# Forward transforms of two spectral layers: column units placed between the next group's row units

## The reference, cut to what matters

```python
x_ft = jnp.fft.rfft2(gn(x))          # layer 0: 16 of the 33 half-spectrum columns and 28 rows are used
mix(x_ft[:, :, :K2, :MODES_T], w[0]) # ... and three more blocks of 6 to 8 rows
...
x_f = jnp.fft.rfft2(gn(x))           # layer 3: the whole half spectrum
out_f = jnp.einsum('bchw,ochw->bohw', x_f, k_f)
```

## Time and profile before

| what | us |
| --- | --- |
| median of three runs | 924.1 (920.47 to 928.2) |
| span of the profiled execution | 904.1 |
| median less the span | 20.0 |
| layer 0's transform: first product's result read, to the next stage's first product | 153.89 to 218.05 |
| layer 3's transform: first product, to the end of its last copy | 616.79 to 710.18 |

### The profile page before, as it was taken

One profiled execution on the slowest core, in us unless ns is written; L12 is line 12 of the kernel. 1 busy time (PEld: TensorE's weight loads), 2 busy tenths in 40 slices (PEclk: granted clock), 3 DMA queues, 4 the chain that ended last, 5 costly groups with the idle time before them and its releaser, 6 DMA issues. The chain is left out here.

```text
span 904.1 us, 27651 instructions
## 1 busy us (share of the span) xinstructions
PE 755.6 (84%) x11429; PEld 633.2 (70%) x11429; DVE 586.3 (65%) x1097; ACT 456.1 (50%) x768; POOL 86.2 (10%) x80
## 2 busy tenths in 40 slices
PE   7999997785599667876799999958888498988996
PEld 7999996674588546665344444428777388888996
DVE  3554464777847745887786777776666676765445
ACT  0133336775343305652699995007887556775200
POOL 0000000010010002644022313000000100000000
PEclk9999998998899987997999999988999898999998
DMA  8599878862110000000000000004000447860036
GB/s 309 205 344 350 317 217 253 186 137 43 27 31 0 0 2 1 0 0 1 1 1 2 1 1 1 1 1 95 0 0 0 93 95 162 175 128 1 1 142 236
DMA packets 48668, 80.52 MB, mean 89 GB/s; under 512 B 20034, under 2 KB 38472, under 8 KB 43736
## 3 DMA queue, kind: packets, MB, share of 16 engines
q1 hardware_dynamic: 31960, 62.75, 25.0%
q10 hardware_dynamic: 16640, 16.78, 5.4%
HBM read 51.01 MB, written 27.92 MB: 87 GB/s over the span
## 5 line engine op out<-in xcount | busy, mean ns | idle before, releaser
L1588 DVE SCALAR_TENSOR_TENSOR X<-bank,c_power,X 32x512 f32 x128 | 96.8, 756 | 36.5 <-PE bank L1538 32.8
L1731 PE MATMUL bank<-m_xp,m_kf 128*32 128x64 f32 x2048 | 82.7, 248 | 22.2 <-DVE m_xp L1666 11.1
L1731 PEld LDWEIGHTS bank<-m_xp,m_kf 128*32 128x32 f32 x2048 | 81.4, 171 | 23.5 <-issue 23.5
L220 DVE BATCH_NORM_STATS2 bn<-X 128x6 f32 x128 | 83.1, 683 | 2.9 <-POOL X L1328 1.6
L420 DVE COPY ks_rows<-bank 128x512 f32<-128x512 f32 x64 | 41.2, 687 | 66.6 <-PE bank L350 66.6
L438 ACT COPY ks_spec<-bank 128x512 f32<-128x512 f32 x64 | 34.4, 589 | 97.4 <-PE bank L365 97.4
L1494 ACT ACTIVATE c_r<-X,c_nrm 32x1024 f32 (+1 forms) x56 | 74.9, 1337 | 2.4 <-DVE c_nrm L1562 1.1
L350 PE MATMUL bank<-ks_fw,ks_src 64*128 64x64 f32 x1024 | 68.7, 298 | 6.3 <-DMA ks_src<-in_L_conv_weights 6.3
L350 PEld LDWEIGHTS bank<-ks_fw,ks_src 64*128 64x128 f32 x1024 | 68.1, 215 | 6.2 <-issue 6.2
L365 PE MATMUL bank<-ks_fh,ks_rows 64*128 64x128 f32 (+1 forms) x1152 | 71.5, 279 | 0.0
L365 PEld LDWEIGHTS bank<-ks_fh,ks_rows 64*128 64x128 f32 (+1 forms) x1152 | 67.0, 183 | 2.6 <-issue 1.8
(11 more groups left out here) (183 smaller groups left out, 1683.5 us busy)
## 6 DMA issues: line engine op xcount, KB each, us to landing
ks_src<-in_L_conv_weights SPq DMA_DIRECT2D x16, 1024.0 KB, 7.0
kf<-ks_spec ACTq DMA_DIRECT2D x16, 1024.0 KB, 9.2
m_kf<-kf SPq DMA_DIRECT2D x32, 512.0 KB, 8.5
X<-in_x SPq DMA_DIRECT2D x4, 2048.0 KB, 12.6
out_y<-X SPq DMA_DIRECT2D x32, 256.0 KB, 2.6
xf<-l_y SPq DMA_DIRECT2D x24, 112.0 KB, 2.1
l_wb<-in_L_conv_weights_r SPq DMA_DIRECT2D x4, 512.0 KB, 11.5
l_wb<-in_L_conv_weights_i SPq DMA_DIRECT2D x4, 512.0 KB, 13.4
```

Of the source, the lines that this page charges most:

```text
L220: dve.bn_stats(self.bn[:, c, :], self.X[:, q, c * CH:(c + 1) * CH]).then_inc(step, 1)
L1588: dve.scalar_tensor_tensor(x, of.rearrange("p (y x) -> p y x", x=HN), filt.power[at, 2:3], x, ALU.mult, ALU.add).then_inc(added, 1)
L1731: last = pe.matmul(ps[4 * half + m // 8][at:at + C, m % 8 * N:(m % 8 + 1) * N], kf[p][:, j, :, H * half + m], xp[half][:, j, m].rearrange( ...
```

## The change

A group's column units no longer follow its row units at once. All units of the four groups are put in one list, in which column unit `s` of a group follows the next group's row units by two places. In layer 3 the list begins with eleven row units, goes on with one column and one row in turn, and ends with ten column units (the last two of group 2 and all of group 3). In layer 0 it is eleven row units, then one column unit for every two row units, and five column units at the end (the last of group 2 and the four of group 3).

`f_rows` is there twice. `f_src`, `f_th` and `f_tl` are rings of four units, and `f_ch`, `f_cl` are gone: column units use the same rings. Each engine goes through the list; on ACT and DVE the copy out of the bank of unit n - 4 stands ahead of unit n. Everything is written out without loops.

The normalisation of a chunk goes to POOL, apart from the first group's first three chunks (DVE, DVE, ACT) and, in layer 0, chunk 2 (DVE) and chunk 6 (ACT) of the other groups. Row copies go to ACT for units 1 and 5 in layer 0, 3 and 7 in layer 3, and otherwise to DVE. In layer 3 ACT's copy into `xm` writes four neighbouring elements at a time, where it wrote single ones 32 elements apart.

```diff
-    def __init__(self, pr, ctx, name, mats, slot_at, rows_by_act, norm_by_act, norm_by_dve):
+    AHEAD = 3
+    RING = 4
+    def __init__(self, pr, ctx, name, mats, slot_at, rows_by_act, normal_by):
+        per = NCH // self.S
+        place = {(0, q, j): 2 * (NCH * q + j) for q in range(Q) for j in range(NCH)}
+        place |= {(1, q, s): 2 * (NCH * q + NCH + per * s + 2) + 1 for q in range(Q) for s in range(self.S)}
+        self.units = sorted(place, key=place.get)
...
+        self.src = pr.sb(ctx, f"{name}_src", [P, self.RING, CH])
+        self.th, self.tl = (pr.sb(ctx, f"{name}_{n}", [P, self.RING, CH], F16) for n in ("th", "tl"))
+        self.rows = [pr.sb(ctx, f"{name}_rows{p}", [P, N, 2, 4 * self.S]) for p in range(2)]
...
+    def wait_source_free(self, eng, q, j):
+        m = NCH * q + j - self.RING
+        if m >= 0:
+            eng.wait_ge(self.turned, self.at[0, m // NCH, m % NCH] + 1)
...
+        def multiply(n):
+            kind, q, i = self.units[n]
+            pe.wait_ge(self.turned_read, n + 1)
+            if n >= 4:
+                self.wait_evicted(pe, n - 4)
...
+        turned = 0
+        for n in range(len(self.units)):
+            while turned < min(n + self.AHEAD + 1, len(self.units)) and self.rows_before(turned) <= n:
+                turn(turned)
+                turned += 1
+            multiply(n)
...
+    def normalise(self, eng, e, q, j):
+        pr = self.pr
+        if q >= Q or self.normal_by(q, j) != e:
+            return
+        self.wait_source_free(eng, q, j)
+        to, of = self.src[:, (NCH * q + j) % self.RING], pr.X[:, q, j * CH:(j + 1) * CH]
+        scale, shift = pr.rstd[:, q:q + 1], pr.shift[:, q:q + 1]
+        if e == "act":
+            m = eng.activation(to, of, ACT.Identity, scale=scale, bias=shift)
         else:
+            m = eng.tensor_scalar(to, of, scale, shift, ALU.mult, ALU.add)
+        m.then_inc(self.ready[e], 1)
...
+        for n, (kind, q, i) in enumerate(units):
+            for m in range(evicted, max(evicted, self.rows_before(n), n - self.AHEAD)):
+                evict(m)
+            evicted = max(evicted, self.rows_before(n), n - self.AHEAD)
+            act.wait_ge(self.turned, n + 1)
+            if n >= self.RING:
+                act.wait_ge(self.made, n - self.RING + 1)
...
-                for q in range(Q):
-                    for s in range(S):
-                        pool.wait_ge(fwd.kept, START + S * q + s + 1)
-                        pool.tensor_tensor(xm[q % 2][:, 1, s, :, 0, :],
+                for j in range(fwd.RING):
+                    fwd.normalise(pool, "pool", 0, j)
+                for kind, q, i in fwd.units:
+                    if kind == 0:
+                        fwd.normalise(pool, "pool", *divmod(NCH * q + i + fwd.RING, NCH))
+                    else:
+                        pool.wait_ge(fwd.kept, S * q + i + 1)
+                        pool.tensor_tensor(xm[q % 2][:, 1, i, :, 0, :],
...
-                fwd.high_parts(act, lambda q, s: act.copy(
-                    xm[:, s, :, :, bass.ds(IB * q, IB)].rearrange("p k r b -> p b r k"),
-                    pr.psum[4 + s % 4][:].rearrange("p (b r k) -> p b r k", b=IB, r=2)))
+                fwd.high_parts(act, lambda q, s, bank: act.copy(
+                    xm[:, s, :, :, IB * q:IB * q + IB], bank[:].rearrange("p (b r k) -> p k r b", b=IB, r=2)))
```

More of the change, by code:

```diff
@@ L476, in __init__ @@
[L476 to L484, removed]
+        self.ready = {e: pr.sem(f"{name}_ready_{e}") for e in ("act", "dve", "pool")}
+        self.rows_read = {e: pr.sem(f"{name}_rows_read_{e}") for e in ("act", "dve")}
@@ L495, in product @@
             return pe.matmul(to, l, m[:, 0], start=False, stop=True)
-        pe.sem_inc(self.turned, START)
-        self.pr.keep_warm(pe, 7)
[L499 to L536, removed]
-            for s in range(S):
[L538 to L602, removed]
-        else:
-            for q in range(Q - 1):
-                group(q, True)
-        group(Q - 1, False)
@@ new lines, in multiply @@
+        def multiply(n):
+            kind, q, i = self.units[n]
+            pe.wait_ge(self.turned_read, n + 1)
+            if n >= 4:
+                self.wait_evicted(pe, n - 4)
+            bank, th, tl = ps[4 + n % 4], self.th[:, n % self.RING], self.tl[:, n % self.RING]
+            for k in range(4):
+                at = slice(k * P, (k + 1) * P)
+                w = width if kind else self.RW
+                m = product(bank[:, k * w:(k + 1) * w], th[:, at], tl[:, at], self.fh if kind else self.fw)
+            if kind and i == 0 and self.fh0 is not None:
+                for b in range(IB):
+                    at = slice(b * P, b * P + C)
+                    m = product(bank[0:C, b * width:(b + 1) * width], th[:, at], tl[:, at], self.fh0)
+            m.then_inc(self.made, 1)
@@ new lines, in high_parts, with evict @@
+    def high_parts(self, act, keep):
+        ps, units = self.pr.psum, self.units
+        def evict(n):
+            kind, q, i = units[n]
+            self.copy_rows(act, "act", act.copy, n)
+            if kind:
+                act.wait_ge(self.made, n + 1)
+                keep(q, i, ps[4 + n % 4]).then_inc(self.kept, 1)
+        for j in range(NCH):
+            if j < self.RING:
+                self.normalise(act, "act", 0, j)
+        evicted = 0
+        for n, (kind, q, i) in enumerate(units):
[3 more added lines that the diff above has]
+            act.wait_ge(self.turned, n + 1)
+            if n >= self.RING:
+                act.wait_ge(self.made, n - self.RING + 1)
+            if kind == 0:
+                act.copy(self.th[:, n % self.RING], ps[n % 4][:]).then_inc(self.high, 1)
+                self.normalise(act, "act", *divmod(NCH * q + i + self.RING, NCH))
+            else:
+                act.copy(self.th[:, n % self.RING].rearrange("p (b s c) -> p s b c", b=IB, s=4),
+                         ps[n % 4][:].rearrange("p (s b c) -> p s b c", s=4, b=IB)).then_inc(self.high, 1)
+        for n in range(evicted, len(units)):
+            evict(n)
@@ L711, in _, with keep @@
             def _(act):
-                def keep(q, s):
+                def keep(q, s, bank):
                     if s == 0 and q >= 2:
```

126 lines of the change are left out of this document (79 added, 47 removed).

## The result

The changed kernel takes **896.0 us** (median of 4, 883.61 to 899.71) against 925.27 for the kernel before on the same chip: ratio 0.961, 95% interval 0.953 to 0.969. Faster, and by more than I forecast: 29 us by the medians where the sum had 23, and 36 by the ratio, which leaves out the longer of a kernel's executions. The steps that led to the forecast were off by more, in both directions.

A forecast was written before the change was run, and what follows sets the result against it. No engine is full; time is lost at seams between phases and in phases another engine paces. Span 904.1 less 12.1 (layer 3) and 10.9 (layer 0) is 881.1, plus 20.0 around it 901.1 us; range 893 to 915.

The forecast's parts named there:

- The 20.0 that lie around it: Whole execution: 20.0 us lie around the span, added to the forecast span of 881.1.
- A gain of 12.1 us: Layer 3's forward transforms: 93.4 us before, 81.3 after; bounds of the gain 6 to 15.
- the pair: Layer 3: one row and one column unit cost PE 2.34 us, plus 0.1 misfit for each of 21 pairs.
- A gain of 10.9 us: Layer 0's end: the next stage's products start at 207.1 in place of 218.05.
- All of it passes on: Stage after layer 0's transform: keeps the whole 10.9 us, as PE paces it to its last products.
- The triple: Layer 0: two row units and one column unit take 2.65 us (2.47 to 2.95), PE and DVE close.
- POOL's chunk: Normalising one chunk on POOL takes 0.9 us (0.4 to 2.54), off the path at any price below 1.35.
- Code without loops ... at nothing: PE's written-out code: fetching costs 0.43 us per unit's 16 products, under a unit's 0.82, so nothing; at most 2 us.
- the old phases' 1.25: Rival, only the seams go: layer 3's 60 units at 1.25 us, gains 7.3 and 8, total 908.8; chance 0.15.
- POOL was never the bound: Rival: POOL's chunk at 2.54 us paces both layers, total 931; chance 0.08, shared with other net costs.
- SyncE's wait: Rival: layer 0's triple keeps 3.75 us, loads land at 217.8, nothing gained there, total 912; chance 0.10.
- The case with hardly a misfit: Whole kernel: better than the forecast, with hardly any misfit of pairs; chance 0.05.

The follow-up runs named there:

- `s_seams`: Changed kernel with each group's columns directly behind its rows, and no new-phase unit transposed until the last phase is multiplied: 892.86 us, layer 3 86.0.

## Why the prediction was right or wrong

**"The 20.0 that lie around it"** failed, and is the largest error. Only 1.8 to 2.2 us lie around a span (899.71 and 897.6; in the repeated runs 889.26 and 887.1, 932.44 and 930.6). The 20 between the profile of before and its median were the clock in the last stage: the profiled execution kept 2.4 GHz until the last 42 products of it, 84.4 us; of the three other profiled executions with the first place after product 86, all dropped at it (107.0, 104.3, 104.8). Of the 14 profiled with the first place elsewhere none dropped at it; ten took 81.8 to 86.0, and four of those after 65 dropped later (90.7 to 94.3, the profile after among them). The change moved the place by 21 products, which is worth some 18 us, and nothing in the prediction looked at that. It could have: a trace of 904.1 in a kernel of 924 asks for the stage in which the others lose the rest. Between two profiles in which the clock was low at most at the very end of that phase, 904.1 and 887.1, the change gives 17.0 us where the sum has 23.0. That 901.1 came within 6 us of the median is luck: layer 0 gave some 9 less than forecast, layer 3 some 4 more, and the place 18 that the sum doesn't have, 36 in all, as the repeated medians have it (926.26 and 889.55).

**"A gain of 12.1 us"** in layer 3: right in its mechanism as to the end state, PE as the bound, and too small: 15.9 (by the sum's own interval, 615.32 to 693.04, it is 77.7 us where the sum has 81.3). The term is the pair, 2.34 and 0.1 of misfit; it measured 2.28, so 21 pairs cost 21 x 0.16 = 3.4 less. DVE's and ACT's loads, the new copy (0.5, measured 0.50) and the wait at the first column unit (0.9, 0.7 to 0.9) were as forecast. What was wrong is which part gives it. The sum put it all on the alternation that fills seams; the runs give the alternation 1 to 2, the breaks 2, the copy 7 in the kernel before, GpSimd 5 in the serial order. The parts stand in for each other, since each takes load off ACT or DVE where these pace PE or gives PE other work meanwhile. The 0.83 that the earlier trace rows show for the copy was the price to look at in the kernel before, too. The Trainium skill's rule on 16-byte lines ("SBUF — State Buffer", the first door, the DMA port swizzle), by which runs of four are cheap, agrees with the 1087 and 585 ns, though the order of the reads changed together with that of the writes, and no run parts the two.

**"A gain of 10.9 us", "All of it passes on"** in layer 0: both failed. The mix starts 3.5 earlier: group 0 is negated at 176.4 instead of 173.3 (its first column unit waited 2.20, not 0.55, and the layer began 0.8 later), and SyncE's three groups take 35.3 instead of 31.3, its stores at 4.29 and 4.83 and its loads at 5.99 twice, against 3.58 and 5.24. Those two are the prices of the last group; for the stores of its first two groups the trace of before already had 4.59 and 4.03. Why they are slower there no run shows. Of the 3.5, the stage's end keeps 1.1 (243.5 against 244.6), or 1.9 counted from the start of the layer (98.2 against 100.1). PE's 128 products take 2.3 to 2.4 us with the clock at 0.50 as at 1.00; what differs is the gap after them, up to 1.69 now against 1.12 before. The repeated run of before has up to 1.65, so this varies with the execution, not only with the change. The triple itself was good: group 2's last negation began at 193.70 (forecast, with its end, 193.5).

**POOL's chunk** took 0.775 us (0.9), off the path at every point; DVE does the same operation in 0.54, so GpSimd is 1.4 times slower with one tensor read. The Trainium skill's "roughly line-rate" for one input ("GPSIMD Engine Reference", Engine selection) is thus kinder than this trace. **"Code without loops ... at nothing"** was right for the transforms, whose units are long enough, and wrong for what follows: it is the length of that code that moved the place (layer 0's alone from 86 to 127, layer 3's alone to 24, so by +41 and -62 products, and both by -21, to 65).

**Of the rivals** none came: layer 3's units ran at PE's 1.14, not at the old phases' 1.25, POOL was never the bound, and SyncE's wait took most of layer 0's gain though the triple ran at 2.5, and 2.7 on the average of a group, not at 3.75. The case with hardly a misfit, which had a chance of 0.05, is what layer 3 showed.

## What to carry to other kernels

Before a median is split into span and overhead, subtract a timed execution's own span from its own time; when the profile is faster than the median, some stage of the other executions is slower, and that stage may pay for an edit anywhere. An edit that changes the length of an engine's written-out code moves the places at which later code is fetched; when the time moves by more than the edited stage, shift the code with instructions that do nothing, allow for their own time, and see. Of a change with several parts, undo them one at a time and also all together: parts that relieve the same engine hide each other, and the cheapest one, here the order of one copy, may give nearly half.

## What the runs showed of the hardware

A semaphore instruction of PE takes 0.153 us when many stand in a row (214 in 32.8 us). A stall of 1.15 us between small products left the clock at 1.2 GHz for the 50 us behind it, in which the products were back to back and PE was busy 5.00 of 5.00. After gaps of 0.62, 0.64, 0.76 and 1.15 it fell; after others of 0.75 (before, 884.06) and 0.76 (`s_seams`, 874.38) and the 0.77 that every kernel waits for ACT ahead of the phase it didn't. So the size of the gap alone doesn't decide; what does stays open.
